# A one-core decoder layer in fp32: attention folds on 64 rows of the array, other banks for the first attention, the bias in the folded weights, and the last down product in token order

## The chip, the cores and the metric

The kernel is one program on 1 core of one Trainium2 chip. The time is the device time of one execution in microseconds (us); less is better. The times of a kernel are shown as the median of its runs with the lowest and the highest. One execution is profiled as well, and all rows of the trace come from that one.

## What is computed

One decoder layer on `x` of 4 x 256 tokens with 128 channels (1024 tokens, eight tiles of 128), all in fp32. Three blocks follow one another, each with a norm ahead and a residual behind:

```python
# 1. windowed self-attention: windows of 32 tokens, 16 heads of 8, causal
qkv = xg @ w_qkv; q = rmsnorm(q, ln_w); k = rmsnorm(k, ln_w)
att = softmax(mask(q @ k.T / sqrt(8))); x = x + (att @ v) @ w_proj
# 2. cross-attention to a context of 64 rows per batch, 16 heads of 64
xn = layernorm(layernorm(x)) * gamma + beta
q = xn @ w_q; k, v = split(ctx @ w_kv)
x = x + (softmax(q @ k.T / 8) @ v @ w_out + b_out) * tanh(gate)
# 3. experts: router with groups (2 of 4), 4 of 16 experts, and 2 shared ones
y = einsum('etf,efd->etd', silu(x @ gate_w[e]) * (x @ up_w[e]), down_w[e])
x = x + einsum('etd,te->td', y, combine) + shared(x)
```

## The kernel before, in words

The program is written engine by engine, with semaphores between them; each engine does its instructions in the order in which they are written, and these orders are long lists of calls by hand (`transpose_qk(4)`, `fold(("kv", 4))`, ...). The changed lists are the order in which the work of the eight token tiles is laced together.

**First attention, tile t.** TensorE turns the normed tile (`transpose_xn`), projects it (`project_qkv`, `project_v`), turns q and k, and computes the scores of four windows and 16 heads with 16 matmuls on 32x32 tiles of the array (`scores1`, L1485) into columns 0 to 127 of the banks 0 to 3 (`wide`). VectorE masks and subtracts the maximum (`mask1`, `max1_sub`), ScalarE takes the exponential, TensorE turns it (`transpose_p1`, L1495), multiplies by v (`values1`, L1503), VectorE divides (`norm_y`), TensorE turns the result (`project_y`, L1510) and projects it (`project_out`, L1517), and VectorE adds the residual. The last four steps all use bank 7 (`PV`). GpSimd builds the block matrix `kbd` from k and the two norm factors.

**Folding of the second attention.** Since the context is short, the kernel doesn't compute q, k and v of the second attention for each token. It multiplies the weights by the context once: for each pair of heads j (eight pairs) a `kv` unit computes k and v of the pair for all four batches (L1540), an `A` unit multiplies `wqT` by k (L1547) into `qk_fold`, and a `VW` unit multiplies v by `w_out` (L1555) into `vo_fold`. These units are laced into the first attention. A pair of heads takes 128 rows, 64 each. So that both heads can be multiplied on the whole array, k and v are stored in `k2` and `v2` with a block of zeros for the other head: GpSimd clears v2 (L538), VectorE k2 (L1220), and ScalarE copies each `kv` unit in four pieces of 64 rows (L742). The results are copied by ScalarE (L746, L748, the latter with tanh(gate) as scale). All units but the odd `VW` ones go through bank 6 (`FOLD`).

**Second attention, tile t.** `scores2` (L1570) is two matmuls of 512 columns into two of the banks 0 to 3; VectorE takes the maximum, subtracts it (L1056, L1060), ScalarE takes the exponential (L765), VectorE sums (L1065), GpSimd multiplies by the reciprocal (`norm_p2`, L457), TensorE turns the result in two halves (L1584), ScalarE copies them (L772), and `output2` adds one matmul of one row (ones by the scaled bias, L1597) and eight matmuls with `vo_fold` (L1599) in bank 5; VectorE adds the residual.

**Experts.** Tokens go in two chunks of 512. x is split in two fp32r parts by ScalarE and VectorE, the gate and up weights by GpSimd (`split_hi`, `split_lo`, L548, L553). For each of 18 experts and chunk there are a gate and an up product of three matmuls each (L1629 to L1631), SiLU on ScalarE (L800), a product on VectorE (L1227), for routed experts a second one with the token's weight (`weigh`, L1235), and one `down` (L1671) that accumulates in bank 6 or 7 with features on the partitions. The routing is some 25 small VectorE instructions; the weights then go to memory and come back spread over all partitions (SP queue, L394, L388). The gate and up weights are loaded in the place of `v2` when the folds are done. At the end of a chunk ScalarE copies the sum (L806), TensorE turns its four tiles (`turn_y`, L1678), VectorE adds them to x (L1241) and SP stores 256 KB.

## Time and profile before

| | us |
|---|---|
| median of 3 runs | 205.37 |
| lowest, highest | 205.02, 209.54 |
| profiled execution | 205.46 |
| its span, first to last instruction | 203.4 |

| engine | busy, us | share of the span |
|---|---|---|
| TensorE, matmuls | 188.0 | 92% |
| TensorE, weight loads | 132.0 | 65% |
| VectorE | 140.1 | 69% |
| ScalarE | 100.2 | 49% |
| GpSimd | 90.3 | 44% |

The mean granted clock of TensorE is 0.987. The first attention lies at about 7 to 60 us of the span, the second at 60 to 115, the experts from 108 to the end. In a row of the order of time, a matmul's own duration overlaps the next one's, so what it costs is the time from its start to the start of the next row. An fp32 matmul has two records, and x8 means four matmuls; turns and the expert products have one.

### The profile page before, as it was taken

How to read it: one execution, taken by the hardware profiler on the slowest of the kernel's cores; microseconds unless marked ns; L12 is line 12 of the kernel's file. 1: busy time of each engine (PE TensorE's matmuls, PEld its weight loads, DVE VectorE, ACT ScalarE, POOL GpSimd, SP SyncE). 2: the span in 40 equal slices, each digit the busy share in tenths (PEclk: the TensorE clock that was granted, in tenths of full speed). 3: DMA queues.
4: the chain of work that ended last, by engine and by line, in shares of the span. 5: the costliest groups of instructions: out<-in, count | busy, mean ns of one | idle time of the engine just before them, and what ended most of it. 6: DMA issues, size and time to landing. Idle time of an engine off the chain costs nothing.

```text
span 203.4 us, 4505 instructions
## 1 busy us (share of the span) xinstructions
PE 188.0 (92%) x1597; PEld 132.0 (65%) x1597; DVE 140.1 (69%) x303; ACT 100.2 (49%) x241; POOL 90.3 (44%) x175
## 2 busy tenths in 40 slices
PE   6767998999999999999989999899999999999991
PEld 6635566577576877777778867456666675766640
DVE  2846655776497878889798975978598438554761
ACT  2266897888956685464546746032223233222201
POOL 4465365546279288887786799910000000000000
PEclk9988999999999999999999999999999999999998
DMA  4980000000052049000000003533630054624401
GB/s 122 342 213 0 3 3 5 3 3 3 3 153 55 3 135 266 15 0 2 3 0 0 0 5 109 168 142 122 189 108 0 2 147 147 214 85 135 148 9 52
DMA packets 16791, 15.83 MB, mean 78 GB/s; under 512 B 1777, under 2 KB 12418, under 8 KB 16642
## 3 DMA queue, kind: packets, MB, share of 16 engines
q1 hardware_dynamic: 16770, 15.56, 25.2%
q8 instruction: 13, 0.21, 0.5%
q14 instruction: 8, 0.07, 0.1%
HBM read 14.96 MB, written 0.59 MB: 76 GB/s over the span
## 4 chain that ended last, share of the span: by engine, by line
PE 65%; POOL 11%; ACT 8%; DVE 5%; issue 3%; DMA 3%; SPq 2%; POOLq 0%; ACTq 0%
PE bank L1671 13%; PE wide L1629 6%; PE wide L1631 6%; PE wide L1630 6%; PE wide L1570 6%; PE bank L1599 6%; POOL gu_lo L553 5%; PE bank L1547 4%; PE bank L1540 3%; DMA beta_col<-in_L_xattn_ln_beta_dram 3%; POOL gu_hi L548 3%; ACT k L742 3%; ACT v L742 3%; PE bank L1584 2%; PE bank L1555 2%
## 5 line engine op out<-in xcount | busy, mean ns | idle before, releaser
L800 ACT ACTIVATE kbd<-wide 128x512 f32<-128x512 f32 x36 | 21.4, 598 | 51.3 <-DVE p L1227 18.3
L1629 PE MATMUL wide<-x3hi,gu_lo 128*128 128x512 f32 x72 | 38.1, 529 | 0.3 <-POOL gu_lo L553 0.3
L1631 PE MATMUL wide<-x3hi,gu_hi 128*128 128x512 f32 x72 | 28.6, 397 | 0.0
L1630 PE MATMUL wide<-x3lo,gu_hi 128*128 128x512 f32 x72 | 28.5, 395 | 0.0
L1227 DVE TENSOR_TENSOR s<-kbd,wide 128x512 f32<-128x512 f32 x18 | 12.3, 684 | 11.4 <-PE wide L1631 5.7
L1629 PEld LDWEIGHTS wide<-x3hi,gu_lo 128*128 128x128 f32 x72 | 13.6, 189 | 8.8 <-issue 5.9
L1227 DVE TENSOR_TENSOR p<-kbd,wide 128x512 f32<-128x512 f32 x18 | 12.3, 684 | 9.9 <-PE bank L1671 5.8
L1630 PEld LDWEIGHTS wide<-x3lo,gu_hi 128*128 128x128 f32 x72 | 13.6, 189 | 7.1 <-issue 5.3
L457 POOL TENSOR_TENSOR p<-p,rs 128x1024 f32<-128x1024 f32 x8 | 15.2, 1901 | 6.6 <-DVE rs L1069 6.5
L1671 PE MATMUL bank<-vbd,wq_sb 128*128 128x512 f32 x32 | 16.2, 601 | 0.6 <-DVE vbd L1235 0.6
L1599 PE MATMUL bank<-vo_fold,p2T 128*128 128x128 f32 x128 | 16.7, 282 | 0.0
L517 POOL TENSOR_TENSOR kbd<-qkT,hmask 128x512 f32<-128x512 f32 x8 | 10.0, 1256 | 13.3 <-ACT qkT L705 13.2
L1599 PEld LDWEIGHTS bank<-vo_fold,p2T 128*128 128x128 f32 x128 | 15.1, 192 | 1.1
L1631 PEld LDWEIGHTS wide<-x3hi,gu_hi 128*128 128x128 f32 x72 | 13.5, 188 | 3.2
L1671 PE MATMUL bank<-vbd,wqT 128*128 128x512 f32 x32 | 15.5, 593 | 0.0
L1570 PE MATMUL wide<-qk_fold,xn2T 128*128 128x512 f32 x32 | 15.3, 601 | 0.0
L1235 DVE TENSOR_TENSOR vbd<-s,wkv_sb 128x512 f32<-128x512 f32 x16 | 11.4, 720 | 3.2 <-PE bank L1671 2.2
L553 POOL TENSOR_TENSOR gu_lo<-v,gu_hi 128x256 fp32r<-128x256 f32 x16 | 12.4, 794 | 0.2
L772 ACT COPY p2T<-bank 128x512 f32<-128x512 f32 x16 | 9.2, 578 | 6.7 <-PE bank L1584 6.7
L1547 PE MATMUL bank<-k,wqT 128*128 128x256 f32 x32 | 9.4, 402 | 2.8 <-ACT v L742 2.7
L1235 DVE TENSOR_TENSOR vbd<-p,wkv_sb 128x512 f32<-128x512 f32 x16 | 11.7, 754 | 0.4 <-PE bank L1671 0.4
L1056 DVE TENSOR_REDUCE mx<-wide 128x16 f32<-128x1024 f32 x8 | 9.7, 1215 | 2.9 <-PE wide L1570 2.7
(157 smaller groups left out, 391.1 us busy)
## 6 DMA issues: line engine op xcount, KB each, us to landing
wkv_sb<-w_rows SPq DMA_DIRECT2D x32, 256.0 KB, 3.3
wkv_sb<-in_L_xattn_w_kv_dram SPq DMA_DIRECT2D x1, 1024.0 KB, 7.0
v<-in_L_ffn_gate_w_dram SPq DMA_DIRECT2D x4, 256.0 KB, 4.4
v<-in_L_ffn_up_w_dram SPq DMA_DIRECT2D x4, 256.0 KB, 5.8
wq_sb<-in_L_xattn_w_q_dram SPq DMA_DIRECT2D x1, 512.0 KB, 4.7
wout_sb<-in_L_xattn_w_out_dram SPq DMA_DIRECT2D x1, 512.0 KB, 6.4
wq_sb<-in_L_ffn_down_w_dram SPq DMA_DIRECT2D x1, 512.0 KB, 3.9
wqT<-in_L_ffn_down_w_dram SPq DMA_DIRECT2D x1, 512.0 KB, 5.1
```

The lines of the kernel that those rows point to most:

```text
L457: pool.tensor_tensor(p2[:, t % 3, :, :], p2[:, t % 3, :, :], rs2[:, t % 2, :].unsqueeze(2).to_broadcast([P, H2, CTX]), ALU.mult).then_inc( ...
L553: pool.tensor_tensor(gu_lo[:, n, :, :], gu_of(n), gu_hi[:, n, :, :].bitcast(F32), ALU.subtract).then_inc(wsplit_lo, 1)
L800: sc.activation(sil[:, k % 2, :], bank[up_bank(k)], ACT.Silu).then_inc(sil_s, 1)
L1227: dve.tensor_tensor(act[k % 4], sil[:, k % 2, :], bank[up_bank(k) + 1], ALU.mult).then_inc(g_s, 1)
L1235: dve.tensor_tensor(aw[k % 3], act[k % 4], spread[:, r % SPREAD, :, :].rearrange("p t q -> p (t q)"), ALU.mult).then_inc(awv_s, 1)
L1547: last = pe.matmul(FOLD[:, m * B * CTX:(m + 1) * B * CTX], wqT[:, j, :], k2[:, j % 2, bs, :, :].rearrange("p b h s -> p (b h s)"), start=T ...
L1570: last = pe.matmul(wide[:, scores_bank(t) + n, :], xn2T[:, t % 2, :], fold_b[:, n * 512:(n + 1) * 512], start=True, stop=True)
L1599: last = pe.matmul(OUT2[:, 0:D], p2T[:, j, :], vo_fold[:, j, b, :], start=False, stop=(j == NPAIR - 1))
L1629: pe.matmul(dst, lo, x3hi[:, cols], start=True, stop=False)
L1630: pe.matmul(dst, hi, x3lo[:, cols], start=False, stop=False)
L1631: return pe.matmul(dst, hi, x3hi[:, cols], start=False, stop=True)
L1671: pe.matmul((FOLD, PV)[c], dn_of(n), rhs, start=(n == 0), stop=(n == NE - 1)).then_inc(y_s, 1)
```

## The change

Four things are changed, and with them the orders of all engines.

1. **Folds on 64 rows.** k2 and v2 become one tile `kv` without zeros. The query-key fold of a pair is one matmul per head on rows 0 to 63 and one on 64 to 127. The value-out fold takes two pairs at once: 16 matmuls of 64 rows by 64 columns, four per pair and batch couple, that write halves of the partitions of two banks. For the batches 2 and 3 the two heads of a pair change places in both folded tensors. The clearing of zeros goes.
2. **Other banks in the first attention.** y's turn, the projection and the query-key folds use columns 128 on of the banks 0 to 3; a list of turns says how they alternate with scores1. The score banks of the second attention and the expert products swap roles.
3. **The bias** is loaded into all partitions, scaled, and added to the first head's rows of `vo_fold` by GpSimd; the eight one-row matmuls go.
4. **The last expert of the second chunk** is multiplied in token order: the sum of the others is copied and turned by matmul into four banks, and four matmuls add the last product there. Four adds and four stores of 64 KB follow, from two queues.

```diff
-                    sc.wait_ge(v2_zero, j + 1)
-                    for m, dst in enumerate((k2, v2)):
-                        for h in range(2):
-                            hs = slice(DH * h, DH * (h + 1))
-                            last = sc.copy(dst[hs, j % 2 if m == 0 else j, :, h, :],
-                                           FOLD[hs, m * B * CTX:(m + 1) * B * CTX].rearrange("p (b s) -> p b s", b=B))
+                    sc.copy(kv[:, j, :, :, :].rearrange("p n b s -> p (n b s)"), FOLD[:, :]).then_inc(f_copied, 1)
+            def copy_A(j, h):
+                sc.wait_ge(a_ready, j + 1)
+                sc.copy(fold_slot(h, j), wide[:, 2 + h, P:P + B * CTX].rearrange("p (c b s) -> p c b s", c=2, b=2)
+                        ).then_inc(a_copied, 1)
...
+            def fold_A(j):
+                pe.wait_ge(f_copied, unit_no[("kv", j)] + 1)
+                if wide_before(("A", j), "scores"):
+                    pe.wait_ge(sm1_s, wide_before(("A", j), "scores"))
+                if j >= 1:
+                    pe.wait_ge(a_copied, 2 * j)
+                for h in range(2):
+                    rows = slice(DH * h, DH * (h + 1))
+                    last = pe.matmul(wide[:, 2 + h, P:P + B * CTX], wqT[rows, j, :],
+                                     kv[rows, j, 0, :, :].rearrange("p b s -> p (b s)"), start=True, stop=True)
+            def fold_VW(g):
...
+                for j in range(2):
+                    for b in range(2):
+                        for c in range(2):
+                            for h in range(2):
+                                rows = slice(DH * h, DH * (h + 1))
+                                slot = (h + c) % 2
+                                col = (2 * j + b) * D
+                                last = pe.matmul(VW_BANKS[g][c][CTX * slot:CTX * (slot + 1), col:col + D],
+                                                 kv[rows, 2 * g + j, 1, 2 * c + b, :], wout_sb[rows, 2 * g + j, :],
+                                                 start=True, stop=True)
...
             def scores1(t):
+                for kind, done, each in (("y", yT_s, 1), ("out", res1_s, 1), ("A", a_copied, 2)):
+                    if wide_before(("scores", t), kind):
+                        pe.wait_ge(done, each * wide_before(("scores", t), kind))
             def transpose_p1(t):
-                    pe.wait_ge(res1_s, t)
+                    pe.wait_ge(yn_s, t)
             def project_out(t):
-                pe.matmul(PV[:, 3 * P:4 * P], yT[:, :], wproj_sb[:, :], start=True, stop=True).then_inc(o1_s, 1)
+                pe.matmul(wide[:, 1, P:2 * P], yT[:, :], wproj_sb[:, :], start=True, stop=True).then_inc(o1_s, 1)
...
-                    pe.matmul(OUT2[:, 0:D], ones_row[:, :], bias_out[:, :], start=True, stop=False)
+            def add_bias():
+                head0 = vo_fold[0:CTX, 0, :, :]
+                pool.tensor_tensor(head0, head0, bias_b[0:CTX, :].unsqueeze(1).to_broadcast([CTX, B, D]),
+                                   ALU.add).then_inc(bo_r, 1)
...
+            def turn_last():
+                pe.wait_ge(yc_s, 2)
+                for m in range(TPC):
+                    pe.matmul(LAST[m][:, 0:D], y_sb[:, m * P:(m + 1) * P], ident[:, :], start=True, stop=False)
+            def down_last():
+                pe.wait_ge(*weighted(k))
+                for m in range(TPC):
+                    pe.matmul(LAST[m][:, 0:D], aw[k % 3][:, m * P:(m + 1) * P], dn_of(NE - 1),
+                              start=False, stop=True).then_inc(last_s, 1)
...
-            keep_busy(14)
-            keep_busy(10)
+            keep_busy(12)
```

The first place is TensorE in the middle of the first attention, around tile 4: first the rows of before, then those of the changed kernel. L1547 is the query-key fold before and L1595 after, L1485 and L1522 are scores1, L1540 and L1580 the k and v of a pair, L1517 and L1560 the projection.

```order
L1474 MATMUL bank4<-ident,qkn 128x128 x2
L1540 MATMUL bank6<-ctxT,wkv_sb 128x256 x2
L1447 MATMUL bank4<-ident,xn 128x128
L1503 MATMUL bank7<-vbd,p1T 32x36 x16
L1466 MATMUL bank4<-wqkv_sb,xnT 32x32 x16
L1455 MATMUL bank5<-wqkv_sb,xnT 128x256
L1510 MATMUL bank7<-ident,yn 128x128
L1547 MATMUL bank6<-k2,wqT 128x256 x2
L1517 MATMUL bank7<-wproj_sb,yT 128x128
L1485 MATMUL wide<-kbd,qkT 32x128 x16
```

```order
L1508 MATMUL bank4<-ident,qkn 128x128 x2
L1580 MATMUL bank6<-ctxT,wkv_sb 128x256
L1481 MATMUL bank4<-ident,xn 128x128
L1550 MATMUL wide<-ident,yn 128x128
L1595 MATMUL wide<-kv,wqT 128x256 x2
L1489 MATMUL bank5<-wqkv_sb,xnT 128x256
L1560 MATMUL wide<-wproj_sb,yT 128x128
L1500 MATMUL bank4<-wqkv_sb,xnT 32x32 x16
L1522 MATMUL wide<-kbd,qkT 32x128 x16
L1532 MATMUL bank7<-ident,p1 128x128 x4
```

The fold has left bank 6, y and the projection have left bank 7, and all of them now stand in `wide` between two scores1; the two halves of a k and v unit stand apart.

The second place is TensorE between the two attentions, again before and then after. L1555 is the value-out fold before and L1617 after, L1570 and L1635 are scores2, L1584 and L1649 the turns of the second attention, L1597 the bias, L1599 and L1663 the output.

```order
L1555 MATMUL bank6<-wout_sb,v2 128x128 x4
L1517 MATMUL bank7<-wproj_sb,yT 128x128
L1555 MATMUL bank5<-wout_sb,v2 128x128 x4
L1570 MATMUL wide<-qk_fold,xn2T 128x512 x2
L1584 MATMUL bank6<-ident,p2 128x128 x4
L1447 MATMUL bank4<-ident,xn 128x128
L1584 MATMUL bank7<-ident,p2 128x128 x4
L1597 MATMUL bank5<-bias_out,ones_row 128x128
L1599 MATMUL bank5<-vo_fold,p2T 128x128 x8
```

```order
L1560 MATMUL wide<-wproj_sb,yT 128x128
L1481 MATMUL bank<-ident,xn 128x128
L1635 MATMUL wide<-qk_fold,xn2T 128x512 x2
L1617 MATMUL bank<-wout_sb,kv 64x128 x16
L1635 MATMUL wide<-qk_fold,xn2T 128x512 x2
L1617 MATMUL bank<-wout_sb,kv 64x128 x16
L1635 MATMUL wide<-qk_fold,xn2T 128x512 x2
L1481 MATMUL bank<-ident,xn 128x128
L1649 MATMUL bank<-ident,p 128x128 x8
L1663 MATMUL bank<-vo_fold,p2T 128x128 x8
```

Four scores2 stand ahead of the first turn of the second attention instead of three, the value-out groups stand between them, and nothing stands between the turns and the output.

The third place is the end of TensorE's order. L1671 and L1735 are downs, L1678 and L1752 the turns of the sum, L1759 the last expert in token order.

```order
L1631 MATMUL wide<-x3hi,gu_hi 128x512
L1671 MATMUL bank<-vbd,wqT 128x512
L1629 MATMUL wide<-x3hi,gu_lo 128x512
L1630 MATMUL wide<-x3lo,gu_hi 128x512
L1631 MATMUL wide<-x3hi,gu_hi 128x512
L1671 MATMUL bank<-vbd,wqT 128x512 x5
L1678 MATMUL bank<-ident,y_sb 128x128 x4
```

```order
L1735 MATMUL bank<-vbd,wqT 128x512
L1693 MATMUL wide<-x3hi,gu_lo 128x512
L1694 MATMUL wide<-x3lo,gu_hi 128x512
L1695 MATMUL wide<-x3hi,gu_hi 128x512
L1735 MATMUL bank<-vbd,wqT 128x512
L1752 MATMUL bank<-ident,y_sb 128x128 x3
L1752 MATMUL wide<-ident,y_sb 128x128
L1759 MATMUL bank<-wqT,vbd 128x128 x3
L1759 MATMUL wide<-wqT,vbd 128x128
```

One down stands behind the last product instead of five, then the turns and the four matmuls of the last expert.

## Rows read from the trace of the kernel before

**Rows 1.** Busy time of each engine by stretches, all engines.
```profile
core 0: us, PE busy (x) PEld busy (x) DVE busy (x) ACT busy (x) POOL busy (x), PEclk, DMA share, GB/s
13.80:17.30 3.50, 3.50 (x71) 2.29 (x70) 2.24 (x5) 1.62 (x8) 2.02 (x4) 0.53 0.31 76
20.00:60.00 40.00, 37.43 (x753) 26.02 (x752) 26.11 (x59) 32.74 (x103) 20.79 (x37) 1.00 0.05 14
60.00:75.00 15.00, 14.85 (x152) 11.30 (x151) 11.51 (x19) 10.36 (x19) 10.02 (x20) 1.00 0.22 60
75.00:105.00 30.00, 29.67 (x191) 23.08 (x190) 25.83 (x45) 15.78 (x34) 24.41 (x42) 1.00 0.22 62
105.00:133.00 28.00, 26.40 (x129) 18.28 (x127) 22.85 (x59) 15.11 (x30) 24.24 (x40) 1.00 0.19 58
133.00:190.00 57.00, 56.75 (x205) 38.08 (x205) 37.12 (x81) 15.71 (x28) 0.25 (x1) 1.00 0.35 112
```

**Rows 2.** Order of time, TensorE, one query-key fold: start, us, instruction.
```profile
41.02 1.03 PE L1547 MATMUL bank<-k,wqT 128*128 128x256 f32 x4
41.89 0.60 PE L1495 MATMUL bank<-ident,p 128*128 128x128 f32 x4
```

**Rows 3.** Order of time, TensorE, scores1 and one value-out fold.
```profile
58.01 0.50 PE L1485 MATMUL wide<-kbd,qkT 32*32 32x128 f32 x32
58.44 1.16 PE L1555 MATMUL bank<-wout_sb,v 128*128 128x128 f32 x8
59.43 0.60 PE L1495 MATMUL bank<-ident,p 128*128 128x128 f32 x4
```

**Rows 4.** Groups by line: busy us, mean ns, idle before and its cause.
```profile
L742 ACT COPY k<-bank 64x256 f32<-64x256 f32 x16 | 5.9, 366 | 0.9 <-PE bank L1540 0.7
L746 ACT COPY qk_fold<-bank 128x512 f32<-128x512 f32 x8 | 4.7, 588 | 0.4 <-PE bank L1547 0.2
L517 POOL TENSOR_TENSOR kbd<-qkT,hmask 128x512 f32<-128x512 f32 x8 | 10.0, 1256 | 13.3 <-ACT qkT L705 13.2
L1547 PE MATMUL bank<-k,wqT 128*128 128x256 f32 x32 | 9.4, 402 | 2.8 <-ACT v L742 2.7
```

**Rows 5.** Order of time, ScalarE and TensorE, the start.
```profile
12.08 0.47 ACT L705 ACTIVATE qkT<-bank,lnw_col 128x256 f32<-128x256 f32 x1 [0.23 <-DMA beta_col<-in_L_xattn_ln_beta_dram]
17.42 0.74 ACT L742 COPY k<-bank 64x256 f32<-64x256 f32 x2 [0.74 <-PE bank L1540]
18.18 0.74 ACT L742 COPY v<-bank 64x256 f32<-64x256 f32 x2
...
18.97 0.70 PE L1547 MATMUL bank<-k,wqT 128*128 128x256 f32 x2 [1.37 <-ACT v L742]
```

**Rows 6.** Order of time, TensorE, one tile of the second attention.
```profile
78.37 1.88 PE L1570 MATMUL wide<-qk_fold,xn2T 128*128 128x512 f32 x4
...
80.52 0.33 PE L1447 MATMUL bank<-ident,xn 128*128 128x128 f32 x1
80.78 0.48 PE L1597 MATMUL bank<-bias_out,ones_row 1*128 1x128 f32 x2
81.19 2.05 PE L1599 MATMUL bank<-vo_fold,p2T 128*128 128x128 f32 x16
...
83.66 1.10 PE L1570 MATMUL wide<-qk_fold,xn2T 128*128 128x512 f32 x2
```

**Rows 7.** Order of time, VectorE, from one residual to the next.
```profile
78.02 0.29 DVE L1075 TENSOR_TENSOR x<-bank,x 128x128 f32<-128x128 f32 x1 [0.67 <-PE bank L1599]
...
83.28 0.29 DVE L1075 TENSOR_TENSOR x<-bank,x 128x128 f32<-128x128 f32 x1 [0.51 <-PE bank L1599]
```

**Rows 8.** Order of time, all engines, the end of the program.
```profile
194.15 4.49 PE L1671 MATMUL bank<-vbd,wqT 128*128 128x512 f32 x10
198.67 0.58 ACT L806 COPY y_sb<-bank 128x512 f32<-128x512 f32 x1 [5.14 <-PE bank L1671]
...
200.00 0.69 DVE L1241 TENSOR_TENSOR x<-bank,x 128x512 f32<-128x512 f32 x1 [2.81 <-PE bank L1678]
200.72 0.39 SPq L398 DMA_DIRECT2D out_dram<-x  x1
```

More of the change, by code:

```diff
@@ L356, in scores_bank, with wide_before, fold_slot @@
         def scores_bank(t):
-            return 2 * (t % 2) if t < TPC else 0
-        UNITS = [("ctx", 0), ("wq", 0), ("wq", 1)] + [(kind, j) for j in range(NPAIR - 1) for kind in ("kv", "A")] + \
-            [("kv", NPAIR - 1), ("A", NPAIR - 1)] + [("VW", j) for j in range(NPAIR)]
+            return 2 * ((t + 1) % 2) if t < TPC else 2
+        UNITS = [("ctx", 0), ("wq", 0), ("wq", 1)] + [("kv", j) for j in range(NPAIR)]
         unit_no = {u: n for n, u in enumerate(UNITS)}
-        def fold_bank(u):
-            return QK if u[0] == "VW" and u[1] % 2 == 1 else FOLD
+        VW_BANKS = [(FOLD, QK), (PV, FOLD), (QK, PV), (FOLD, QK)]
+        WIDE_TURNS = [("scores", 0), ("A", 0), ("scores", 1), ("y", 0), ("A", 1), ("out", 0), ("scores", 2),
[3 rows of a table added]
+                      ("out", 7)]
+        def wide_before(turn, kind):
+            return sum(k == kind for k, _ in WIDE_TURNS[:WIDE_TURNS.index(turn)])
+        def fold_slot(h, j):
+            half = qk_fold[:, 0, j, h * CTX:(h + 1) * CTX]
+            pair = 2 * INNER + (CTX if h == 0 else -CTX)
+            return bass.AP(half.tensor, half.offset, [half.ap[0], [pair, 2], [INNER, 2], [1, CTX]])
         block = ctx.enter_context(nc.Block())
@@ L1352, in _ @@
             norm_stats(2, 7)
-            multiply(1)
+            split_x3(4)
             split_x3(5)
@@ L1536, in fold @@
                                             ident[:, :])
-                elif kind == "kv":
+                else:
                     pe.wait_ge(wkv_l, 16)
-                    for m in range(2):
+                    for m in halves:
                         last = pe.matmul(FOLD[:, m * B * CTX:(m + 1) * B * CTX],
@@ L1712, in _ @@
+            project_qkv(3)
+            fold(("kv", 2), halves=(1,))
             project_out(0)
-            project_qkv(3)
-            fold(("kv", 2))
-            scores1(2)
             transpose_p1(1)
             project_v(3)
-            fold(("A", 2), halves=(0,))
-            fold(("A", 2), halves=(1,))
+            scores1(2)
+            values1(1)
             transpose_qk(3)
-            values1(1)
-            fold(("kv", 3))
+            fold_A(2)
             transpose_xn(0, 4, T1[:, 0:P])
+            project_y(1)
@@ L1940, in _ @@
             up(27)
+            down(23)
             up(28)
```

745 lines of the change are left out of this document (380 added, 365 removed), and 3 rows, old and new, of the table WIDE_TURNS.

## The prediction

> **What bounds the kernel now.** I read the busy time by stretches first, then TensorE's order of time inside one tile of each attention, then the waits, then the end. TensorE is busy 37.4 of 40 us in the first attention, 14.9 of 15 us where the value folds lie, 29.7 of 30 us in the second attention and 56.8 of 57 us in the expert stage; no other engine is above 33 of 40 [rows 1]. So a microsecond of TensorE work taken out before 133 us comes back as time, as long as the next engine leaves room. That next engine is ScalarE in the first attention (32.7 of 40) and VectorE in the second (25.8 of 30) [rows 1]. The expert stage itself (72 three-matmul products, 36 downs) keeps its work, so the gain has to come from the 105 us ahead of it and from the last few us.
>
> **The change part by part, in us of TensorE unless said.**
>
> *Query-key fold, 8 times.* Before, one fold is two 128x256 matmuls on the whole array: 41.02 to 41.89, 0.87 [rows 2]. Half of what they multiply are zeros. After, there are still two matmuls of 256 columns, one on rows 0 to 63 and one on rows 64 to 127, into two banks. Whether they run together is not in the trace for 64 rows; the nearest row is scores1: 16 matmuls of 128 columns on 32x32 tiles take 0.43 from start to the next instruction [rows 3], while four 128-column matmuls of the whole array take 0.99, 0.25 each [rows 3]. So tiles do overlap: 16 in turn would be 4.0. Of the 0.43, one matmul's stream is about 0.22 (0.87 / 2 for 256 columns, halved), and 0.21 is the way into and out of the small tiles. A fold then costs 0.43 + 0.21 = 0.64, a gain of 0.23, 1.8 for eight. Bounds: no way in and out gives 0.44 each, 3.4 gained in all; no overlap gives 0.87 + 0.21 each, 1.7 lost.
>
> *Value-out fold.* Before: 8 times four matmuls, 0.99 each [rows 3], 7.9. After: four groups of 16 matmuls of 64 rows by 64 columns, four of which can stand on the array at once. A group is four rounds of 0.22 plus 0.21, 1.09; four groups 4.4; gain 3.5. I take 3.0, because the PE order puts the last groups between score matmuls that wait for VectorE (11.5 of 15 busy there [rows 1], so 3.5 is just about all the room there is). The bounds are 3.5 and, with matmuls one after another at 0.25, 64 x 0.25 = 16, a loss of 8.
>
> The Trainium skill (TensorEngine Tiling (Array Packing), Gotcha 1: PSUM Pressure) says that different row tiles cannot access one PSUM bank at the same time. The two row halves of each value-out pair write one bank, on different partitions. In the trace the row tiles of scores1 go to four different banks, so nothing here shows that case. By that rule this term would be near 0, by the row it is 3.5; rival 1 prices it.
>
> *Copies on ScalarE.* Per pair of heads, four 64x256 copies (366 ns each) become one 128x512 of about 588 ns, and one qk_fold copy of 588 ns becomes two of 256 columns, about 366 ns each: 2.05 becomes 1.32, 0.7 less per tile, 5.9 in all [rows 4]. It is worth time where TensorE waits for it: 1.37 at the first fold, whose four copies take 0.74 + 0.74 [rows 5]; 1.48 - 0.59 = 0.9 of this goes, I take 0.8. Elsewhere the named waits are 2.7 less these 1.37 [rows 4]. The first attention has 2.6 idle in 40 [rows 1]; with ScalarE going from 8.2 to about 7 tenths I give back 0.9 of it. Bounds 0 and 2.0.
>
> *Second banks.* The turn of y and the projection move from bank 7, which also holds p1T and the values, to free columns of the four score banks. TensorE's work is the same. The next tile's p1 transposes now wait for the normed y and no longer for the residual. In exchange scores1, A, y and out take turns on these banks (rival 3). I cost it at nothing: one round of turns is 0.43 scores, 0.7 mask, 0.64 fold, 0.73 copies, and about 0.9 for y, its copy, out and residual, 3.4, under the 5.7 or so that a tile takes (40 us for 7 tiles). All of it hides under TensorE's other work; without that cover each turn adds.
>
> *Bias.* The eight one-row matmuls go: 80.78 to 81.19, 0.41 each [rows 6], 3.3. In their place GpSimd scales 128x128 and adds 64x512 once. The nearest row is its 128x512 product, 1256 ns [rows 4]; I take 1.2 for the add (bounds 0.6 and 1.3) in a stretch where GpSimd is busy 10.0 of 15 and has lost two splits (1.3), which now stand earlier. VectorE limits how much of 3.3 is kept: its round is 78.02 to 83.28, 5.26, with 0.51 idle [rows 7], so it needs 4.75; TensorE's tile is 78.37 to 83.66, 5.29 [rows 6], and would be 4.88. There is room, but only 0.13. The orders also pull gate 0 and up 0 a tile earlier into what is left. I take 2.7 (bounds 1.0 and 4.0, the latter if the longer step ahead of the one-row matmul goes too: 80.52 to 80.78 for a transpose, 0.26).
>
> *Cleared zeros.* Eight memsets on GpSimd and two on VectorE go; both engines are idle there, nothing on the path.
>
> *Start.* 12 instead of 24 warming transposes. The first real work moves up by 2 us, but ScalarE's first qkT still waits for the beta column at 12.08 [rows 5], in the same place of the queue, and so does all behind it. Half of the wq transposes is then already done (0.4 gained). Against that TensorE is at the lower level from about 13.8 to 17.3 (0.53 of full speed over that stretch [rows 1]) after a thin stretch; less work ahead may lengthen this. Net: 0.3 lost, bounds +0.4 gained and 1.7 lost.
>
> *End.* Let T be the end of the last product. Before, two more downs of 0.86 follow (in truth five stand there in a row, 194.15 to 198.64 with the last one's run-out of about 0.16 [rows 8]), and from the end of the last stream, 198.48, it is 4.9 to the end at 203.4: copy, turns, one add of 0.69, one 256 KB store that starts at 200.72 and takes 2.7 to the end [rows 8]. T + 6.6. After: down 34 ends at T + 0.9, the copy of the sum of the others at T + 1.6, four turns by matmul take 1.0, four token-order matmuls 1.0, with four adds of 0.28 behind them one by one; the last ends about T + 4.2. Its store, a quarter of the bytes, is issued by ScalarE; 2.7 less an allowance of 0.4, so T + 6.5. I count 0.1 gained, bounds 0.5 lost and 0.6 gained. The last expert's weighting hides behind down 34, the copy and the turns.
>
> **Sum.** 0.8 + 1.8 + 0.9 + 3.0 + 2.7 + 0.1 - 0.3 = 9.0. The profiled execution took 205.46 (span 203.4 and 2.06 around it), beside a median of 205.37: 205.46 - 9.0 = 196.5.
>
> **Rivals.**
> 1. *The 64-row halves don't overlap where they share a bank.* For: no row shows it. Against: scores1 and the column tiles overlap fully. Value-out gain 0: 196.5 + 3.0 = 199.5. If nothing overlaps: 1.8 + 1.7 and 3.0 + 8 more, 211; the rows on 32x32 tiles speak against that.
> 2. *The next engines bind.* VectorE's round leaves 0.13, and the way from the second attention over routing, the row store and the spread load to the first weighted down goes through VectorE, 22.9 of 28 busy [rows 1]. TensorE can't run ahead of that down by more than the buffers. Then half of 9.0 is kept: 201.0.
> 3. *The turns on the score banks become the path (the other side).* ScalarE and VectorE work in order; if each of six hand-overs of a round waits for one foreign instruction of 0.6, a round is 3.4 + 3.6 = 7.0 instead of 5.7: +1.3 x 8 = 10.4, and the 2.7 of the first attention are lost: 196.5 + 2.7 + 10.4 = 209.6. It decides from a round of about 6.5 on, where the other gains are eaten. Against it: the order of the rows leaves two or three instructions between most neighbours.
> 4. *The change doesn't do what it says:* folds cheaper only on paper, because the copies set their pace, and the bias a wait on GpSimd ahead of the first p2: 203 (within 2%).
>
> **Chances.** Forecast 0.66; rival 1 0.08 (0.01 of it the bad form); rival 2 0.15; rival 3 0.04; rival 4 0.07. The range: downwards the upper bounds, 0.9 + 3.4 + 2.0 + 3.5 + 4.0 + 0.6 + 0.4 = 14.8 or 190.7, of which I take 192.5, as all of them at once is unlikely; upwards it takes in rival 1 and rival 2, 201.0. What is left out holds about 0.2. About 2% is what this kernel's runs can tell from no change (201.3 is the line): faster 0.84 (the forecast, rival 1's mild form, 0.11 of rival 2), same 0.12 (the rest of rival 2, rival 4, 0.01 of rival 3), slower 0.04.
>
> **What would show it.** A fold starting 0.6 to 0.7 before the next instruction; 16 value-out matmuls in about 1.1 (right), 2 (shared bank) or 4 (no overlap). Second-attention tiles of 4.9 and VectorE without idle. The first weighted down some 8 earlier than before. The prediction is wrong if TensorE's idle in 20 to 60 grows over 2.6, if its wait at the first weighted down exceeds 2, or if the clock stays at the lower level past 18.

## The result and the profile after

The changed kernel takes 200.12 us, the median of four runs (199.62 to 202.14), beside 205.75 for the kernel before (205.02 to 209.54): a ratio of 0.975, 95% interval 0.970 to 0.980 (one execution of the kernel before, 209.54, was in a slower state, and the ratios here leave such ones out). That is faster by more than 2%, and inside the forecast range of 192.5 to 201.0; the forecast itself, 196.5, was 3.6 too low. The profiled execution took 199.62 with a span of 197.5 us, against 205.46 and 203.4: 5.9 less, where the sum had 9.0.

The busy time by stretches, which answers to [rows 1]:

```profile
core 0: us, PE busy (x) PEld busy (x) DVE busy (x) ACT busy (x) POOL busy (x), PEclk, DMA share, GB/s
...
20.00:60.00 40.00, 37.58 (x791) 24.02 (x791) 28.80 (x62) 29.28 (x96) 22.33 (x43) 1.00 0.07 19
60.00:75.00 15.00, 14.04 (x199) 8.92 (x197) 12.82 (x21) 10.28 (x18) 9.26 (x17) 1.00 0.30 81
75.00:105.00 30.00, 28.82 (x189) 22.37 (x188) 27.07 (x50) 20.30 (x40) 25.19 (x43) 1.00 0.16 45
105.00:133.00 28.00, 25.40 (x117) 17.88 (x116) 26.23 (x61) 12.94 (x27) 20.48 (x31) 1.00 0.28 89
```

ScalarE fell from 32.7 to 29.3 us in the first attention. TensorE is busy for less of each stretch from 60 to 133 us than it was (14.0 for 14.9, 28.8 for 29.7, 25.4 for 26.4), and VectorE for more. So the stretch in which TensorE's saved work should have become time now has holes in it. The first weighted down starts at 124.7, where it was at 129.7: 5 us earlier, and the forecast had some 8.

The changed operations, in TensorE's order of time (start, us, instruction): a query-key fold, a value-out group, and one tile of the second attention. They answer to [rows 2, 3, 6].

```profile
30.49 0.70 PE L1595 MATMUL wide<-kv,wqT 64*128 64x256 f32 x4
31.12 0.33 PE L1481 MATMUL bank<-ident,xn 128*128 128x128 f32 x1
...
59.85 1.10 PE L1617 MATMUL bank<-wout_sb,kv 64*64 64x128 f32 x32
60.89 0.33 PE L1481 MATMUL bank<-ident,xn 128*128 128x128 f32 x1
...
78.37 1.96 PE L1663 MATMUL bank<-vo_fold,p2T 128*128 128x128 f32 x16
80.17 1.04 PE L1649 MATMUL bank<-ident,p 128*128 128x128 f32 x8
81.66 0.33 PE L1481 MATMUL bank<-ident,xn 128*128 128x128 f32 x1 [0.45 <-POOL xn L484]
```

A fold takes 0.63 from its start to the next instruction (0.87 before), a value-out group 1.04, and no one-row product is left. Between the turn of the probabilities and the transpose at 81.66 stands a new wait of 0.45 for GpSimd.

The end of the program, all engines, which answers to [rows 8]:

```profile
191.14 1.02 PE L1735 MATMUL bank<-vbd,wqT 128*128 128x512 f32 x2
192.20 0.59 ACT L823 COPY y_sb<-bank 128x512 f32<-128x512 f32 x1 [0.26 <-PE bank L1735]
...
193.83 0.83 PE L1759 MATMUL bank<-wqT,vbd 128*128 128x128 f32 x6
...
194.80 0.87 ACTq L827 DMA_DIRECT2D out_dram<-x  x2
194.92 0.29 DVE L1273 TENSOR_TENSOR x<-wide,x 128x128 f32<-128x128 f32 x1
```

From the end of the last product, 191.14, to the end of the span it is 6.4, where the forecast had 6.5 (and 6.6 before).

**Three stretches.** Three stations are easy to find in every trace: the first turn of p1 (the transpose of the first tile's probabilities), the last scores1 of the first attention, and the end of the span. The table has the start of the first, and the two distances behind it. I use them for all experiments, since they separate what happens at the start, which differs from one execution to the next, from the rest.

| kernel | first p1 turn at | to the last scores1 | from there to the end |
|---|---|---|---|
| before | 20.13 | 37.88 | 145.39 |
| changed | 21.77 | 32.76 | 142.98 |
| forecast for changed | 20.4 | 34.4 | 139.6 |

The forecast's row: 0.3 lost at the start; 0.8 + 1.8 + 0.9 = 3.5 gained in the first attention; 3.0 + 2.7 + 0.1 = 5.8 behind it. By the stations, 1.6 were lost, 5.1 gained and 2.4 gained: -1.3, +1.6 and -3.4 against the forecast, in sum the 3.1 by which the profiled execution lies above it.

But the orders have changed, and the stations don't divide the same work. In the changed kernel half of a k and v unit and the third tile's query and key products stand ahead of the first turn of p1; before they stood behind it:

```profile
20.69 0.60 PE L1580 MATMUL bank<-ctxT,wkv_sb 128*128 128x256 f32 x2
21.23 0.70 PE L1489 MATMUL bank<-wqkv_sb,xnT 128*128 128x256 f32 x2
21.77 0.65 PE L1532 MATMUL bank<-ident,p 128*128 128x128 f32 x4
...
56.00 0.70 PE L1595 MATMUL wide<-kv,wqT 64*128 64x256 f32 x4 [0.37 <-issue]
```

What TensorE had done at 20.13 before it has done at 20.69 now, so by equal work the start lost 0.6 and not 1.6. And the last query-key fold (56.00 to the next instruction at 56.76) has moved behind the last scores1. By equal work the three are then 0.6 lost, 3.3 gained and 3.2 gained, which is -0.3, -0.2 and -2.6 against the forecast: nearly the whole miss lies in the last stretch. Among the variants of the changed kernel the order is one and the same, and there the stations compare as they stand. The experiments take the three stretches in turn.

### The profile page after: what moved, and what is told of

It is laid out like the page before. It is cut to its first block, busy times and chain, and to the rows that moved or that the text cites. A ratio compares the mean times of both kernels' runs of the same rounds, so it can differ in the third digit from the quotient of the medians.

```text
span 197.5 us, 4609 instructions
## 1 busy us (share of the span) xinstructions
PE 181.1 (92%) x1643; PEld 123.2 (62%) x1643; DVE 143.2 (73%) x304; ACT 95.5 (48%) x227; POOL 86.6 (44%) x167
## 4 chain that ended last, share of the span: by engine, by line
PE 68%; POOL 9%; DVE 6%; ACT 5%; issue 4%; DMA 4%; SPq 2%; POOLq 0%; DVEq 0%; ACTq 0%
PE bank L1735 14%; PE wide L1693 7%; PE wide L1695 7%; PE wide L1694 7%; PE wide L1635 6%; PE bank L1580 4%; DMA beta_col<-in_L_xattn_ln_beta_dram 4%; PE bank L1663 3%; POOL gu_lo L576 3%; PE wide L1595 3%; PE bank L1489 2%; PE bank L1617 2%; PE wide L1522 2%; POOL p L476 2%; PE bank L1481 2%
## 5 line engine op out<-in xcount | busy, mean ns | idle before, releaser
L1693 PE MATMUL wide<-x3hi,gu_lo 128*128 128x512 f32 x72 | 39.1, 544 | 0.6 <-POOL gu_lo L576 0.6
L1663 PE MATMUL bank<-vo_fold,p2T 128*128 128x128 f32 x128 | 16.8, 278 | 0.8 <-DVE x L1106 0.5
L476 POOL TENSOR_TENSOR p<-p,rs 128x1024 f32<-128x1024 f32 x8 | 15.2, 1902 | 4.4 <-DVE rs L1100 4.4
L1663 PEld LDWEIGHTS bank<-vo_fold,p2T 128*128 128x128 f32 x128 | 15.4, 192 | 2.3 <-issue 1.6
L1735 PE MATMUL bank<-vbd,wq_sb 128*128 128x512 f32 x32 | 16.1, 595 | 0.3 <-DVE vbd L1262 0.3
L1635 PE MATMUL wide<-qk_fold,xn2T 128*128 128x512 f32 x32 | 15.5, 608 | 0.4 <-DVE x L1080 0.4
L1735 PE MATMUL bank<-vbd,wqT 128*128 128x512 f32 x30 | 14.6, 592 | 0.0
L536 POOL TENSOR_TENSOR kbd<-qkT,hmask 128x512 f32<-128x512 f32 x8 | 9.1, 1133 | 11.5 <-ACT qkT L721 11.5
L576 POOL TENSOR_TENSOR gu_lo<-kv,gu_hi 128x256 fp32r<-128x256 f32 x16 | 13.1, 836 | 0.1
L1053 DVE TENSOR_TENSOR s<-wide,causal 128x512 f32<-128x512 f32 x8 | 5.5, 692 | 7.4 <-PE wide L1522 7.3
```

The source lines that it names most:

```text
L476: pool.tensor_tensor(p2[:, t % 3, :, :], p2[:, t % 3, :, :], rs2[:, t % 2, :].unsqueeze(2).to_broadcast([P, H2, CTX]), ALU.mult).then_inc( ...
L576: pool.tensor_tensor(gu_lo[:, n, :, :], gu_of(n), gu_hi[:, n, :, :].bitcast(F32), ALU.subtract).then_inc(wsplit_lo, 1)
L1635: last = pe.matmul(wide[:, scores_bank(t) + n, :], xn2T[:, t % 2, :], fold_b[:, n * 512:(n + 1) * 512], start=True, stop=True)
L1663: last = pe.matmul(OUT2[:, 0:D], p2T[:, j, :], vo_fold[:, j, b, :], start=(j == 0), stop=(j == NPAIR - 1))
L1693: pe.matmul(dst, lo, x3hi[:, cols], start=True, stop=False)
L1735: pe.matmul((FOLD, PV)[c], dn_of(n), rhs, start=(n == 0), stop=(n == NE - 1 or k == NK - 2)).then_inc(y_s, 1)
```

## The experiments

All are edits of the changed kernel, but for one of the kernel before. The times are medians; a ratio is to the kernel before, run on the same chip beside it (the changed kernel's is 0.975). The stations are those of one profiled execution of each kernel.

### The first attention: the copies

**Four copies again.** `copy_fold` in the changed kernel:

```diff
-  sc.copy(kv[:, j, :, :, :]..., FOLD[:, :])
+  for m in range(2):
+      for h in range(2):
+          last = sc.copy(kv[hs, j, m, :, :]..., FOLD[hs, m * B * CTX:(m + 1) * B * CTX])
```

> The changed kernel with each of its four key-and-value copies out of the fold bank written as four copies of 64 rows x 256, as many instructions as the kernel before had. ScalarE gets some 1.2 us more for each pair, 4.9 in all, between 14 and 40 us. Theory (much of the 5.1 us gained from 20 to 54 us is ScalarE's, which the forecast priced at 0.8): first-attention milestones (last scores tile of the first attention, 54.53 in the changed kernel) 1.4 to 2.5 us later, time 201 to 202.5. Rival (the folds on TensorE made all of the gain): under 0.7 us later, time about 200.3.

Measured: 205.08 us, ratio 0.996 (0.991 to 1.001). Nearly the whole gain is gone. The stations are 22.73, 38.26 and 143.17: 5.5 more between the first turn and the last scores1, and only 0.2 behind it. Not all of the 5.5 are the copies', for in this execution TensorE's lower clock lasted until 25.8 (in the changed kernel until 20.5): from the first turn of p1 to the values of that tile the same products take 3.29 us here and 2.05 there. Without these 1.2 the copies cost 4.3, and the ratios say the same (0.996 less 0.975 of 205.75 is 4.3). The expectation, at most 2.5, was too small by two fifths or more, and its working was off: ScalarE's groups by line in the first attention (busy us, mean ns, idle before) show what one copy of a unit and four come to; the first row is the changed kernel's, the second this one's.

```profile
L754 ACT COPY kv<-bank 128x512 f32<-128x512 f32 x8 | 4.8, 595 | 0.9 <-PE bank L1580 0.9
```

```profile
L757 ACT COPY kv<-bank 64x256 f32<-64x256 f32 x31 | 11.4, 367 | 2.0 <-PE bank L1585 1.7
```

That is 6.9 us more of ScalarE (the row leaves out one copy; all 32 come to 11.7), and about 4.3 of it was paid. TensorE's waits from the first turn to the last scores1 add up to 5.7 in this kernel; its view of waits (what it waited at and for, us in total, times, longest):

```profile
PE bank L1585 <- ACT kv L757: 1.5, 2, 0.8
PE bank L1545 <- ACT p1T L735: 1.2, 1, 1.2
PE bank L1494 <- ACT xnT L696: 1.2, 2, 0.6
PE wide L1600 <- ACT kv L757: 0.9, 1, 0.9
```

Only 2.4 of these name the copies. The others are ScalarE's later work (p1T, xnT), delayed in its queue by copies that nobody waits for at that moment. In the changed kernel all waits of this stretch are 1.7.

The Trainium skill (VectorE: DVE Perf Modes, the section on the TRN2 errata) gives a ScalarE copy out of PSUM a fixed part of 172 cycles at 1.2 GHz beside one cycle per column: 0.36 us for 256 columns and 0.57 for 512. By that estimate, four copies of 64 rows pay the fixed part four times and use half of the lanes; the rows agree within 5%, 0.367 and 0.595.

**Two copies in the kernel before.** The other way round, the kernel before with two copies for its four (both heads land in one block, so its zero blocks no longer keep the heads apart):

```diff
-  for h in range(2):
-      last = sc.copy(dst[hs, ..., h, :], FOLD[hs, ...])
+  last = sc.copy(dst[:, ..., 0, :], FOLD[:, ...])
```

> The kernel before, with its four 64x256 copies of a key-and-value unit written as two copies of 128x256 (both halves of the rows land in one block, so the zero-block layout is not kept; this is the part that is left out). ScalarE loses 16 copies: 32 x 0.366 = 11.7 us become 16 x 0.385 = 6.2, 5.5 us less; TensorE's work stays as it was. Theory (ScalarE paces the first attention, as the run with four copies suggests, which lost all of the 5.1 us there): 3.5 to 5.5 us faster than the kernel before, last scores tile of the first attention at 53 to 55 instead of 58.01. Rival (the changed kernel gained there by its folds and its second banks, and the four copies hurt only in its order of work): under 1 us faster.

Measured: 202.13, ratio 0.981 (0.975 to 0.987). Stations 20.40, 35.16, 145.33: 2.7 less in the first attention, the rest unchanged. So copies alone, with folds and banks as before, bring 2.7 of the 3.3 that the whole change gained there by equal work, and half of the 5.5 that ScalarE was spared. The theory had 3.5 to 5.5, the rival under 1; the time (3.4 less) is nearly the theory's and the trace lies between the two. The chain of waits shows where they stand on the path. A piece of it from the kernel before, and one from the changed kernel (start, us, what):

```profile
48.54 0.86 PE bank L1540 x4
...
49.84 0.35 ACT k L742
...
50.20 0.37 ACT k L742
...
50.58 0.36 ACT v L742
...
50.96 0.38 ACT v L742
...
51.38 0.70 PE bank L1547 x2
```

```profile
51.21 0.63 PE bank L1580 x2
...
52.06 0.63 PE wide L1595 x4
```

Before, the way from the key-and-value products (L1540) to the fold on them (L1547) leads through all four copies, 1.5 us in a row. In the changed kernel the chain goes from products to fold on TensorE itself.

**The fold's products twice.** `for h in (0, 1, 0, 1)` in `fold_A`, so that TensorE does each query-key fold twice.

> The changed kernel with the products of each of its eight query-key folds issued twice: TensorE gets about 0.43 to 0.6 us more for each, 3.4 to 4.8 in all, between 19 and 57 us. Theory (ScalarE paces the first attention, so the forecast's 1.8 for these folds bought little): under 2 us slower, time 200.3 to 202. Rival (TensorE paces it, as the forecast had it): 3 to 4.8 us slower, time 203 to 205.

Measured: 201.46, ratio 0.980 (0.976 to 0.983). Stations 21.22, 34.82, 143.59. A doubled fold runs for 1.06 instead of 0.63, 3.4 us more in all; 2.1 was paid in the first attention and 0.6 behind it, where the last fold stands. The time is in the theory's span, but the share paid, eight tenths, is not that of an engine which only waits for ScalarE. Both theories fall in their pure form: in the first attention TensorE and ScalarE stand on the path in turn. An addition to TensorE is paid at about eight tenths, one to ScalarE at about six (4.3 of 6.9), and the relief of ScalarE alone is worth half. The copies (2.7 to 4.3) and the folds (0.24 saved on each of eight, at eight tenths 1.5) come to more than the 3.3 gained by equal work, so something else in the new orders and banks costs 0.9 or more there; no run singles it out.

### Behind the first attention: folds, bias and waits

**The value-out groups twice.** `for j in (0, 1, 0, 1)` in `fold_VW`.

> The changed kernel with the 32 products of each of its four value-out groups issued twice: TensorE gets 4 x 1.03 = 4.1 us more between 59.8 and 71 us. Forecast's theory (the value-out folds stand on TensorE's path, a term of 3.0): 3.3 to 4.1 us slower, time 203.4 to 204.3. Rival (they fill waits of TensorE for the tail of the first attention and the head of the second, so what the change saved there came back as waits): 0.5 to 2 us slower, time 200.6 to 202.

Measured: 202.54, ratio 0.986 (0.981 to 0.991). Stations 21.18, 32.76, 146.43: 3.45 more in the last stretch and none elsewhere. The time by the medians is between the two theories; the stretch says the forecast's. In the order of time a doubled group still runs without a break:

```profile
59.26 1.98 PE L1617 MATMUL bank<-wout_sb,kv 64*64 64x128 f32 x64
61.17 0.33 PE L1481 MATMUL bank<-ident,xn 128*128 128x128 f32 x1
```

A group has 16 products, not the 32 of the expectation; each has two records here. It is 1.91 from start to start for 32 products, 0.87 for the second 16: about 0.22 for each four, where one 128-column product of the whole array takes 0.25 [rows 3]. So four 64x64 quarters of the array run side by side all the time.

**The bias products back.** The one-row products ahead of each output2 tile, and GpSimd's add out:

```diff
+  pe.matmul(OUT2[:, 0:D], ones_row[:, :], bias_b[0:1, :], start=True, stop=False)
...
-  ... start=(j == 0), ...
+  ... start=False, ...
```

> The changed kernel with its eight one-row bias products put back ahead of each output2 tile (a 1x128 ones row against the bias row), and the bias out of the folded rows. TensorE gets some 0.4 to 0.5 us more for each of eight tiles, 3.2 to 4 us in all, GpSimd loses one 1.27 us operation. Theory (VectorE paces the second attention): only +0.5 to +2, first weighted down product at 125.2 to 126.7, time 200.6 to 202. Rival (TensorE paces it): +3 to +4, time 203 to 204, as the forecast's term of 2.7 for the bias had it.

Measured: 202.08, ratio 0.980 (0.971 to 0.989). Stations 21.61, 32.79, 146.05: 3.07 more in the last stretch. The bias term of the forecast, 2.7, holds, and VectorE doesn't pace the second attention in the sense of the theory.

So both terms of the last stretch are real, 3.45 and 3.07, yet the change as a whole won only 2.4 there, 3.2 by equal work. Something else in it costs some 3 us. TensorE's waits show where they went. All of them from 58 to 131 us in the kernel before:

```profile
PE bank L1584 <- ACT p2T L772: 0.8, 1, 0.8
PE bank L1671 <- DVE vbd L1235: 0.6, 1, 0.6
PE bank L1447 <- ACT xn2T L758: 0.2, 1, 0.2
```

and the same part of the program, 54 to 126 us, in the changed kernel:

```profile
PE bank L1481 <- POOL xn L484: 0.8, 2, 0.5
PE wide L1693 <- POOL gu_lo L576: 0.6, 1, 0.6
PE bank L1663 <- DVE x L1106: 0.5, 1, 0.5
PE bank L1673 <- ACT x3T L797: 0.4, 1, 0.4
...
PE wide L1635 <- DVE x L1080: 0.4, 1, 0.4
...
PE wide L1560 <- ACT yT L741: 0.4, 1, 0.4
PE bank L1649 <- POOL p L476: 0.3, 1, 0.3
```

With two more of 0.4 (one for ScalarE, one for nothing the trace names) and three of 0.2 that is 4.8 us where it was 1.6: thirteen waits, of at most 0.6, for GpSimd, VectorE and ScalarE in turn. (The expectation of the last run below has 5.0 for this sum, which is 0.2 too much.) Two of them (yT, and x at L1080) belong to y and the projection, which now take turns with others on the score banks. TensorE's saved 7.6 (3.8 in value-out groups, 3.8 in output2 tiles, start to start) less the 3.2 more of waiting, less 0.8 for the last query-key fold, which has moved into this stretch, leaves 3.6; 2.4 were won. About 1.2 us more sits in single transposes that take longer to hand on, and I can't put a name to it.

**Half the maximum.** VectorE's row maximum over 32 of the 64 keys.

```diff
-  dve.tensor_reduce(mx2[:, t % 2, :], s, AX.X, ALU.max)
+  dve.tensor_reduce(mx2[:, t % 2, :], s[:, :, 0:CTX // 2], AX.X, ALU.max)
```

> The changed kernel, with VectorE's row maximum of the second attention's scores taken over 32 of the 64 keys (softmax subtracts any shift alike, so this is a smaller read and nothing else). One such maximum of a tile gives back about 0.6 us of VectorE, 8 tiles 4.9 us, between 66 and 116 us of the program. Theory (from 70 us on VectorE sets the pace, because GpSimd works beside it): the first weighted down product comes 2 to 3.5 us earlier than in the changed kernel (124.67 there), the time is 197 to 198. Rival (TensorE's own work or the handshakes between the four engines set the pace): under 0.7 us earlier, time 199.5 to 200.

Measured: 199.36, ratio 0.969 (0.959 to 0.979); one maximum fell from 1.20 to 0.66. Stations 20.90, 32.61, 142.96: nothing in the last stretch, the earlier end is the start's. The theory falls: 4.3 us of VectorE, an engine busy for 27 of 30 us, are worth nothing alone.

**Half the normalising.** GpSimd's product of probabilities and reciprocal sums on `0:H2 // 2` of the heads; the other half stays unnormalised.

> The changed kernel with GpSimd's product of the second attention's probabilities with the reciprocal sums over 8 of the 16 heads only (the other 8 are left unnormalised): 1.90 us of GpSimd become about 0.95 for each of eight tiles, 7.6 us in all, between 73 and 107 us. Theory (in the changed kernel GpSimd takes turns with TensorE as the one that sets the pace from 78 us on, since its operations now stand in the chain of waits there): the first weighted down product comes 1.5 to 4 us earlier, time 196 to 198.6. Rival (TensorE sets it): under 0.7 us earlier, time 199.4 to 200.

Measured: 199.80, ratio 0.971 (0.965 to 0.976). Stations 22.42, 33.10, 141.83: 1.15 less in the last stretch for 6.8 us less GpSimd (15.2 to 8.4). More than nothing, less than the theory's 1.5. GpSimd is gone from the chain that ended last, and the sum over the program didn't follow: by engine, this chain is in the changed kernel the first line, here the second.

```profile
PE 68%; POOL 9%; DVE 6%; ACT 5%; issue 4%; DMA 4%; SPq 2%; POOLq 0%; DVEq 0%; ACTq 0%
```

```profile
PE 74%; DMA 8%; ACT 5%; DVE 5%; issue 4%; SPq 3%; POOL 1%; DVEq 0%; ACTq 0%
```

A share of 9% in a chain was thus worth 0.6% of the time.

**Both halves.**

> The changed kernel with VectorE's maximum over half of the keys and GpSimd's normalising product over half of the heads at once (the other 8 heads are left unnormalised), 4.3 us less on VectorE and 7.6 less on GpSimd in the second attention. Each alone gave 0.2 and 0.8 us from the first turn of probabilities to the end. Theory (what was saved on TensorE is given back in waits for several engines in turn, so one engine's relief only hands the wait to the next): together clearly more than the sum of 1.0, 1.5 to 3 us, TensorE's waits from 54 to 126 us (5.0 in the changed kernel, 1.6 in the kernel before) fall under 3.5. Rival (the waits come from ScalarE and from the order of TensorE's own work): at most 1.2 us together.

Measured: 198.44, ratio 0.965 (0.961 to 0.969). Stations 20.63, 32.75, 141.52: 1.46 less in the last stretch, where the two alone gave 0.02 and 1.15. TensorE's waits fell from 4.8 to 4.3, not under 3.5. The time lies between the two, just under the theory's 1.5 and over the rival's 1.2; the waits are not what the theory had. One engine's relief is handed to the next only in small part. Which of ScalarE, the shared banks and TensorE's own order holds the remaining 4.3 wasn't tried, and stays open.

### The start: TensorE's pace

**24 warming transposes instead of 12.**

> The changed kernel with 24 products of keep_busy at the start in the place of 12. Theory (the start lost 1.6 us because its first products after the idle time ran at half the pace): the stretch from 7 to 20.5 us runs at full pace, the turn of the first tile's probabilities is back at 20.1 to 20.5 (21.77 in the changed kernel), time 198.3 to 199. Rival (the pace of the start is a matter of the run, or the start is set by the beta column's load): the half pace stays or the turn stays at 21.5 or later, time 200 or above.

Measured: 198.93, ratio 0.965 (0.953 to 0.976). Stations 21.96, 32.94, 142.98: the turn came no earlier in the profiled execution, which was the slowest of the four (196.8 to 199.7). So in this form the theory isn't borne out, but what the other three did at the start isn't on record. The trace says more. Windows of 2 us of this kernel (columns as above; the third from last is the granted clock):

```profile
10.00:12.00 2.00, 0.83 (x6) 0.64 (x6) 1.81 (x8) 0.74 (x3) 1.23 (x3) 1.00 0.45 110
12.00:14.00 2.00, 0.82 (x3) 0.52 (x3) 0.00 (x0) 1.23 (x3) 1.04 (x1) 0.62 0.99 294
14.00:16.00 2.00, 2.00 (x66) 0.97 (x65) 0.27 (x1) 0.72 (x5) 0.28 (x2) 0.50 0.71 191
...
20.00:22.00 2.00, 2.00 (x8) 1.48 (x7) 0.35 (x1) 1.43 (x4) 0.27 (x1) 0.50 0.00 0
```

With 24 transposes the clock falls at about 13 us, as in the kernel before; with 12 it falls in the window of 8 to 10 us in five of the runs above (to 0.57 of full speed over that window with the doubled fold), and in the others it hadn't risen by then, as the pace of the products below shows. What comes ahead of the fall is in all of them a stretch in which TensorE waits for half of the time or so: for the load of wq, then for ScalarE's qkn and qkT. So I looked at the waits rather than at the beginning.

**The waits filled.**

```diff
+  keep_busy(14)
   fold(("wq", 0), halves=(0,))
   fold(("wq", 0), halves=(1,))
+  keep_busy(12)
   transpose_qk(0)
   fold(("wq", 1))
+  keep_busy(6)
```

> The changed kernel with 14, 12 and 6 more of keep_busy's transposes placed where TensorE waits at the start (ahead of the first wq half, of the turn of the first query and key, and behind the last wq fold), 1.5, 1.3 and 0.7 us at full pace. Nearly all runs so far show 0.50 to 0.65 as the granted clock from about 9 or 13 us to 18 to 24 us, after waits in which TensorE was busy 0.8 to 1.0 of 2 us. Theory (the low pace at the start comes of these waits): the granted clock stays at 1.00 in 8 to 20 us, the turn of the first tile's probabilities comes at 20.0 to 20.8 (20.9 to 22.7 in the runs of the changed kernel and its variants), time 198.3 to 199.3. Rival (the clock falls here whatever TensorE does, or the beta column's load sets this turn): 0.5 to 0.6 as before, the turn at 21 or later, time about 200.

Measured: 196.63, ratio 0.956 (0.953 to 0.959). Stations 18.89, 32.58, 142.95: 2.9 us earlier at the first turn, and nothing else moved. By the time it gave some twice what was expected, and it beats both kernels. Of the 2.9, 0.7 lie ahead of ScalarE's copy of the first turned query and key, which waits for the beta column here too and starts at 12.13 for 12.79; with the same start and no filling it was anywhere from 12.17 to 12.83. The other 2.2 lie behind it: 6.8 us from this copy to the first turn, where the changed kernel took 9.0 and five variants with its start 8.4 to 9.7. TensorE's pace can be read off any product that occurs in all traces, here the two of 256 columns of the second tile's query and key (L1489; start, us). First the changed kernel, then this one:

```profile
14.21 1.22 PE L1489 MATMUL bank<-wqkv_sb,xnT 128*128 128x256 f32 x2 [0.35 <-ACT xnT L696]
```

```profile
13.40 0.70 PE L1489 MATMUL bank<-wqkv_sb,xnT 128*128 128x256 f32 x2 [0.35 <-ACT xnT L696]
```

1.22 against 0.70 is the lower level (1.2 GHz) against the upper one (2.4), with some fixed part in both. In the changed kernel's trace this lasts from the first instruction until 20.5 us. The filled kernel has no product at the lower pace behind 5.5 us.

The Trainium skill (TensorE: Matmul & The Clock Gate, Why this matters for your kernels) wants TensorE kept busy without longer idle gaps for the upper level. The trace agrees as to the direction: the filled waits kept it.

**The two columns first.** The loads of gamma and beta moved ahead of the load of tiles 2 and 3 on SyncE's queue.

> The changed kernel with the loads of the gamma and beta columns issued on SyncE's queue ahead of the load of tiles 2 and 3, where they stood behind it. Theory (the copy of the first tile's turned query and key waits 1.4 us for the beta column): this copy starts at 11.5 to 12.2 instead of 12.79, the time is 0.5 to 1.2 us shorter. Rival (the columns land no earlier, or the tiles that now land later or the wq load take the gain back): within 0.4 us.

Measured: 198.86, ratio 0.967 (0.964 to 0.970). Station 20.53; the others 32.77, 142.96. The copy of the first turned query and key starts at 12.03 and no longer waits for the beta column, as the two rows show, of the changed kernel and of this one:

```profile
12.79 0.47 ACT L721 ACTIVATE qkT<-bank,lnw_col 128x256 f32<-128x256 f32 x1 [1.44 <-DMA beta_col<-in_L_xattn_ln_beta_dram]
```

```profile
12.03 0.47 ACT L721 ACTIVATE qkT<-bank,lnw_col 128x256 f32<-128x256 f32 x1 [0.78 <-PE bank L1508]
```

The first turn is 1.2 earlier than in the changed kernel's profiled execution, of which 0.8 is the copy's; but kernels with one and the same start had the copy at 12.17 to 12.83 and the turn anywhere from 20.6 to 22.4. So the rows show that the wait for the column is gone, and hardly more.

**Both at the start.**

> Both edits of the start in the changed kernel: the filled waits of TensorE and the two columns loaded ahead of tiles 2 and 3. If both theories hold, the turn of the first tile's probabilities comes at 19.3 to 20.0 and the time is 197.5 to 198.7; if neither, about 200.

Measured: 196.34, ratio 0.956 (0.952 to 0.959). Stations 18.42, 32.59, 142.98: 3.35 us earlier than in the changed kernel, but only 0.5 beyond the filled waits alone, and by the ratio no difference from them. With TensorE's waits filled, the columns' earlier arrival is worth little. What the filled waits would give the kernel before, whose clock also falls, wasn't tried.

## Why the forecast came out as it did

**The start, forecast -0.3, measured -0.6 by equal work, -1.6 at the turn of p1.** "Net: 0.3 lost" came out nearly; its bound of 1.7 held, and the text named the sign that came true, a lower level past 18 us. What it missed is what that level costs, and that the waits inside the start decide about it. Filling the waits gave back 2.9, 2.2 of it by pace, and by equal work left the start 2.3 better than in the kernel before (17.81 for 20.13). The filled kernel's 196.63 is close to the 196.5 forecast; this is chance, since its three stretches are not those of the sum. What makes the lower level last until 18 to 26 us in the changed kernel and its variants, where the kernel before [rows 1] is through at 17.3, is open; with two copies the kernel before was through only at 18.8, so part of it may be a matter of the execution.

**The copies, forecast 0.8 + 0.9, worth more.** The mis-sized terms are "I take 0.8" and "I give back 0.9". The forecast had ScalarE's saving at 5.9 and then counted only the waits that name the copies [rows 4, 5]. Undone in the changed kernel they cost about 4.3; made alone in the kernel before they bring 2.7. A copy that nobody waits for still shifts everything behind it in ScalarE's queue, and TensorE's waits for p1T and xnT are the bill. That the first attention came out right in sum (3.3 for 3.5) is luck: the copies were priced too low, and what the new orders cost there, 0.9 or more, was not priced at all.

**Query-key folds, forecast 1.8.** One fold was priced at 0.64 and takes 0.63. At the eight tenths that the doubled folds paid, eight folds are worth 1.5.

**Value-out groups, forecast 3.0.** Priced 1.09, measured 1.03 to 1.04, and of the 3.5 that doubling adds (4 x 0.87) 3.45 was paid. Rival 1 is out: the two row halves that write one bank, on different partitions, run side by side. The Trainium skill (TensorEngine Tiling (Array Packing), Gotcha 1: PSUM Pressure) says that different row tiles cannot access one PSUM bank at the same time. The trace doesn't agree for this form, with 0.22 for each four products; the measurement decides.

**Bias, forecast 2.7.** Put back it costs 3.07. GpSimd's add took 1.27 us, as estimated.

**Second banks, forecast 0, and rival 2.** Here the last stretch lost 2.6 by equal work (3.4 by the stations), nearly all of the miss. The step that failed is the **Sum**: its terms for this stretch were right one by one, but adding them up took for granted that TensorE, with 7.6 us less work, would wait no more than before. It waited 4.8 us where it had waited 1.6. "There is room, but only 0.13" was the warning; rival 2 (the next engines bind) comes nearest to what happened in this stretch, but not by VectorE, whose relief gave nothing. The waits are spread over three engines and thirteen places. Taking work off two of the engines at once gave back 1.5, so what causes the rest of them is read from one trace and not shown. Rival 3 stayed away: the turns on the score banks cost two waits of 0.4, not 10 us.

**The end, forecast 0.1, measured 0.2 to 0.3.** From the last product on, 6.4 for 6.5, beside the 6.6 that the forecast had for the kernel before.

## What to carry to other kernels

Where several engines are within a tenth of the bound, price an edit by the whole work it takes off an in-order queue, not by the waits that name it, and sum the terms of one stretch against the room of the next engines, since terms that are each right don't add up. Undoing one part in the changed kernel and making it alone in the old one give different prices (4.3 and 2.7 here). Before two orders of work are compared by stations, count what stands ahead of each: here the stations alone made the start look 1 us too bad and the first attention 1.8 too good. And look at TensorE's pace at the start: a few idle transposes in its waits gave 3.5 us by the medians, more than half of what the whole change did (5.6).

## What the hardware showed that I had not expected

**The record of the granted clock can be silent.** The page gives the changed kernel a granted clock of 1.00 throughout, yet its products ran at the lower pace until 20.5 us: two of 256 columns took 1.22 us at 6.11 and again at 14.21. Three more executions are like it. With the doubled fold such a pair took 0.70 at 5.93, so the upper level was reached, and 1.22 at 13.74, and the record has the fall between:

```profile
14.00:16.00 2.00, 2.00 (x66) 0.97 (x66) 0.18 (x1) 0.72 (x5) 0.20 (x2) 0.50 0.72 215
```

So the pace of a known product is the better witness.

**A tiny VectorE operation can last as long as GpSimd's big one.** In the changed kernel an operation on 128x16 with two inputs takes 1.84 us, and ends as GpSimd's product does:

```profile
104.88 1.84 DVE L1157 TENSOR_TENSOR r_g<-r_p 128x16 f32<-128x16 f32 x1
...
104.79 1.90 POOL L476 TENSOR_TENSOR p<-p,rs 128x1024 f32<-128x1024 f32 x1 [0.34 <-DVE rs L1100]
```

Where that product is halved to 1.05, the same operation takes 0.98; the next one of its shape (L1158), with GpSimd's product done, takes 0.16.

The Trainium skill (GPSIMD Engine Reference, Specifications) has the memory interfaces shared with VectorE where its instruction has two inputs there; the trace agrees. So VectorE's busy time, 27 of 30 us, holds time in which it is merely held up, which may be one reason why it reads as the bound and isn't.
